# A GpSimd share in the weight split of a mixture-of-experts layer, and an earlier last hidden part

## The chip, the cores and the metric

The kernel runs on one core of one Trainium2 chip. The metric is the device time in microseconds (us) of one execution, the median of several runs. An engine is named here as in the profile: PE is TensorE, DVE is VectorE, ACT is ScalarE, POOL is GpSimd, SP is SyncE (it only issues transfers).

## The reference

Two sub-layers on `x` of 4 x 1024 tokens with 256 numbers each. The first is a cross-attention onto 77 context rows per batch. The second, in which the change lies, is a mixture of nine experts with two picks per token:

```python
x = x + xattn(ctx_1024, layernorm(x), ...)
xf = layernorm(x).reshape(T, H)                          # T = 4096, H = 256
probs = softmax(xf @ Wr)                                 # 9 experts
topk_w, topk_idx = top_k(probs, 2); topk_w /= sum(topk_w)
cw = zeros((T, E)).at[arange(T)[:, None], idxf].add(wf)
gate = silu(einsum('th,ehi->tei', xf, Wg))               # I = 704
hidden = gate * einsum('th,ehi->tei', xf, Wu)
x = x + einsum('tei,eih,te->th', hidden, Wd, cw)
```

## The kernel before

The attention phase (up to about 360 us of the span) sends each token's row to a region of its two experts in device memory. The expert phase then works through 40 tiles of such rows. A **pair** is a tile of 256 rows, a **small tile** one of 128 rows. The small tiles are numbers 6, 11, 16, 20, 25, 30, 34 and 39 of the list `TILES`; 39 is the last of all. So seven small tiles are followed by a pair.

**Number format.** Matmuls run in a rounded float format (`F32R`). To keep precision each operand is split into a rounded part `hi` and a rest `lo = value - hi`, and every product is three matmuls: hi*hi, lo*hi, hi*lo (`product`, lines 341 to 343). ACT makes `hi` (a copy that rounds) and DVE makes `lo` (a subtraction). This holds for the tokens (`tok_t`), for the hidden values (`hid`) and for the weights (`wgt_hi`, `wgt_lo`, made from the loaded `wgt`, or from `spare_wgt` for small tiles).

**Weights of a tile.** They are split in six pieces: `PIECES[0:4]` are gate and up (128 x 704 each), `PIECES[4:6]` are down (128 x 1280, and 128 x 256 of which DVE handles 64 rows). Pieces go two at a time, as parts 0, 1 and 2, through `round_pieces(t, u)` on ACT (line 1113) and `rest_pieces(t, u)` on DVE (line 1961). A tile's pieces are split while the tile ahead of it is computed, into buffer t % 2.

**Order on each engine, written out by hand.**
- PE (`pair_step(t)`): `gate_up(t, 0)`, `gate_up(t, 1)`, `tok_turn(t + 1)` (four transposes, line 1353), `down(t - 1)`, `gate_up(t, 2)`. For a small tile (`single_step(t)`): `single_gate_up(t)`, `tok_turn(t + 1)`, `down(t - 1)`, `hid_turn(t)` (transposes, lines 1471 to 1474).
- ACT and DVE, for each of three inner parts u of a pair: `silu` on ACT, the product `hidden` on DVE (line 1969, for the last part lines 1971 and 1972), weight pieces of tile t + 1, and then the split of the hidden part (`hid_round` on ACT, lines 1148 or 1150 and 1151; `hid_rest` on DVE, lines 1993 or 1996 and 1997). After part 1 the tokens of tile t + 1 are split (`tok_move` line 1098, `tok_rest` line 1945), and ACT writes the result of tile t - 1 (`res_move`, line 1170).
- In a small tile: `single_silu` (line 1142) and `single_hidden` (lines 1981 to 1985), pieces 0, the tokens, pieces 1, `res_move` on ACT, the hidden split (lines 1158 to 1161 on ACT, 2005 to 2008 on DVE), pieces 2.
- POOL, for each tile: `note(t + 2)` (two tiny copies, lines 927 and 928), then `add_results(t)`: wait for the result, one indirect transfer per 128 rows that adds it to the output (line 938), and a wait until these have landed.
- SP: loads of tokens and weights. The down weights of a buffer are loaded anew (`refill_down`) when their split is done.

**What PE waits for.** `gate_up(t, 0)` waits for the first four pieces of tile t (`weights_split`) and for the split tokens (`tok_split`). `down(t)` waits for the last two pieces, for all hidden parts (`hid_ready`) and for a free result bank.

Of the kernel before, what the change touches and what calls it, by code (L numbers as in the profile page):

```python
# [28 lines left out]
P = 128  # L29
# [82 lines left out]
    return 0 if t < EARLY else t % 2  # L112


def pieces_to(t):

    return (t - EARLY) * len(PIECES)

def program(nc, x, ctx_rows, fside, ln1_w, ln1_b, ln2_w, ln2_b, wq, wkv, wout, wr, wg, wu, wd, out):
    valmat_dram = nc.dram_tensor("valmat_dram", (B, H, M, DE), F32).ap()  # L120
# [2 lines left out]
    with ExitStack() as ctx:  # L123
        def sem(name):
            return ctx.enter_context(nc.semaphore(name))
# [321 lines left out]
        tok_split = sem("tok_split")  # L447
        weights_hi = sem("weights_hi")
        weights_split = sem("weights_split")
        hid_made = sem("hid_made")  # L450
        hid_hi = sem("hid_hi")
        pads_zeroed = sem("pads_zeroed")
# [36 lines left out]
            return (early_split, u + 1) if t < EARLY else (weights_split, pieces_to(t) + 2 * KT)  # L489

        def down_split(t):
            return (early_split, UNITS + 2) if t < EARLY else (weights_split, pieces_to(t + 1))

        def tokens_loaded(t):
# [71 lines left out]
        def _(sp):  # L566
# [178 lines left out]
            def refill_down(t):  # L745
                n = TILES[t][1]
                if is_pair(t) and n + WEIGHT_SLOTS < NP:
                    sp.wait_ge(weights_split, pieces_to(t + 1))
                    load_pair_down(n + WEIGHT_SLOTS)
                elif not is_pair(t) and n + 1 < NS:  # L750
                    sp.wait_ge(weights_split, pieces_to(t + 1))
                    load_single_down(n + 1)

            for t in range(EARLY, NT):
# [11 lines left out]
        def _(pool):  # L766
# [163 lines left out]
            for s in range(T + 4):  # L930
                step(s, s)

            def add_results(t):

                i = t % 2
                pool.wait_ge(res_ready, t + 1)
                for a in range(TILES[t][0]):
                    nc.gpsimd.indirect_dma_start(out, bass.IndirectOffsetOnAxis(ap=tok_id[:, t % NOTES, a:a + 1], axis=0),  # L938
                                                 res[i][:, a, :], None, compute_op=ALU.add).then_inc(added, 16)
                pool.wait_ge(added, BLOCKS_TO[t + 1] * 16)  # L940

            pool.wait_ge(tail_row_made, 1)
# [11 lines left out]
        def _(act):  # L954
# [218 lines left out]
            def pair_step(t):  # L1173

                ahead = EARLY - 1 <= t < NT - 1
                src = weights_of(t + 1) if ahead else None
                for u in range(UNITS):
                    silu(t, u)
                    if ahead:
                        round_pieces(t + 1, u, src)  # L1180
                    hid_round(t, u)
                    if u == UNITS - 2 and t:
                        tok_move(t + 1)
                        if t == 2:
                            act.wait_ge(last_stored, 16)
                        res_move(t - 1)

            def single_step(t):

                last = t == NT - 1  # L1190
                src = None if last else weights_of(t + 1)
                single_silu(t)
                if not last:
                    round_pieces(t + 1, 0, src)
                    tok_move(t + 1)
                    round_pieces(t + 1, 1, src)
                res_move(t - 1)
                single_hid_round(t)
                if not last:
                    round_pieces(t + 1, 2, src)  # L1200

            for s in range(T + 4):
                step(s, s)
# [319 lines left out]
        def _(dve):  # L1523
# [487 lines left out]
            def pair_step(t):  # L2011

                src = weights_of(t + 1) if t < NT - 1 else None
                for u in range(UNITS):
                    hidden(t, u)
                    if t < NT - 1:
                        rest_pieces(t + 1, u, src)
                    hid_rest(t, u)
                    if t < NT - 1 and u == UNITS - 2:
                        tok_rest(t + 1)  # L2020

            def single_step(t):
# [6 lines left out]
                    tok_rest(t + 1)  # L2029
                    rest_pieces(t + 1, 1, src)  # L2030
                single_hid_rest(t)
                if not last:
                    rest_pieces(t + 1, 2, src)

            dve.wait_ge(consts_made, 10)
            nc.vector.memset(most[:], 0.0)
# [51 lines left out]
```

## Time and profile before

| | us |
|---|---|
| median of 3 runs (838.15 to 839.69) | 838.44 |
| the profiled execution: its own time | 840.97 |
| the profiled execution: its span, first to last instruction | 839.3 |
| PE busy (95% of the span) | 797.9 |
| DVE busy (80%) | 669.4 |
| ACT busy (74%) | 623.9 |
| POOL busy (45%) | 374.3 |

The span is one execution as the hardware profiler saw it. The execution's own time holds 1.7 us more than the span, around it. Busy shares are averages over phases with different limits; what an engine's idle time costs is seen only where another engine waits for it. In the rows further down, a row without a number in brackets had no idle time worth telling ahead of it. PE's clock was granted in full for nearly all of the span (mean 0.994).

### The profile page before, as it was taken

Reading aid. Unit: us, or ns where it says so; the run is one execution under the profiler, and the core shown is the slowest. Engines: PE = TensorE matmul, PEld = TensorE weight load, DVE = VectorE, ACT = ScalarE, POOL = GpSimd, SP = SyncE. Lnnn points to the kernel's source line nnn. Section 1 sums busy time; section 2 is a strip of 40 time slices with the busy share of each in tenths; the row PEclk is TensorE's granted clock in tenths of the full one; section 3 lists DMA queues with packets and bytes.
Section 4 is the critical chain, followed back from the end, with each engine's and each line's share of the span. In section 5 each row is a group of like instructions: output and inputs, shape, how many; then the busy total and the mean of one; then the engine's idle time right before and its main releaser. Section 6 shows DMA issues by size and latency. Waiting matters only on the chain.

```text
span 839.3 us, 19508 instructions
## 1 busy us (share of the span) xinstructions
PE 797.9 (95%) x6007; PEld 752.6 (90%) x6007; DVE 669.4 (80%) x1624; ACT 623.9 (74%) x1962; POOL 374.3 (45%) x534
## 2 busy tenths in 40 slices
PE   5999999999999999989999999999999999999993
PEld 5846899999999999879999999999999999999993
DVE  6767788888889878888778878788887887888771
ACT  3557889889889888754767777777787777777771
POOL 3020268778777766763324234333333322513232
PEclk9999999999999999999999999999999999999998
DMA  8044731230130121638656283255952654556222
GB/s 288 16 114 134 225 107 39 76 103 27 41 138 30 37 76 39 196 123 203 154 139 161 38 233 77 34 146 149 259 152 46 171 157 113 152 146 158 38 21 25
DMA packets 77675, 96.14 MB, mean 115 GB/s; under 512 B 10311, under 2 KB 64771, under 8 KB 77571
## 3 DMA queue, kind: packets, MB, share of 16 engines
q1 hardware_dynamic: 63811, 75.93, 29.2%
q0 software_dynamic: 13760, 18.96, 12.4%
q8 instruction: 48, 0.79, 0.4%
q14 instruction: 56, 0.46, 0.2%
HBM read 108.14 MB, written 31.29 MB: 166 GB/s over the span
## 4 chain that ended last, share of the span: by engine, by line
PE 83%; DMA 3%; SPq 3%; issue 3%; POOL 2%; DVE 2%; ACT 1%; DVEq 0%; POOLq 0%
PE banks L341 24%; PE banks L342 23%; PE banks L343 23%; PE banks L1339 4%; PE banks L1496 2%; PE banks L1353 2%; PE banks L1295 1%; PE banks L1322 1%; DMA expert_in<-blank 1%; DMA valmat_dram<-val_st 1%; POOL expert_in L875 1%; PE banks L1271 1%; PE banks L1307 1%; SPq L597 1%; DMA wkv_sb<-in_L_xattn_Wkv 0%
## 5 line engine op out<-in xcount | busy, mean ns | idle before, releaser
L341 PE MATMUL banks<-tok_t_hi,wgt_hi 128*128 128x256 f32 x704 | 199.8, 284 | 5.0 <-DVE hid_f L1969 1.9
L343 PE MATMUL banks<-tok_t_hi,wgt_lo 128*128 128x256 f32 x704 | 198.0, 281 | 0.0
L342 PE MATMUL banks<-tok_t_lo,wgt_hi 128*128 128x256 f32 x704 | 197.9, 281 | 0.0
L938 POOL DMA_INDIRECT result<-res,tok_id x72 | 117.7, 1635 | 165.4 <-ACT res L1170 133.8
L1037 ACT ACTIVATE prob<-banks,row_min 128x77 f32<-128x77 f32 x512 | 161.7, 374 | 5.2 <-DVE row_min L1692 5.2
L1961 DVE TENSOR_TENSOR wgt_lo<-wgt,wgt_hi 128x704 fp32r<-128x704 f32 x174 | 150.4, 905 | 14.7 <-ACT wgt_hi L1113 14.7
L341 PEld LDWEIGHTS banks<-tok_t_hi,wgt_hi 128*128 128x128 f32 x704 | 134.3, 191 | 8.1 <-issue 6.0
L343 PEld LDWEIGHTS banks<-tok_t_hi,wgt_lo 128*128 128x128 f32 x704 | 133.6, 190 | 0.0
L342 PEld LDWEIGHTS banks<-tok_t_lo,wgt_hi 128*128 128x128 f32 x704 | 133.4, 190 | 0.0
L1113 ACT ACTIVATE wgt_hi<-wgt 128x704 fp32r (+1 forms) x174 | 130.6, 801 | 0.5
L1037 ACT ACTIVATION_READ_ACCUMULATOR prob<-banks,row_min 128x1 f32 x512 | 130.2, 256 | 0.0
L341 PE MATMUL banks<-wgt_hi,hid_hi 128*128 128x256 f32 x360 | 104.2, 290 | 8.7 <-issue 6.1
L343 PE MATMUL banks<-wgt_hi,hid_lo 128*128 128x256 f32 x360 | 101.3, 281 | 0.0
L342 PE MATMUL banks<-wgt_lo,hid_hi 128*128 128x256 f32 x360 | 101.1, 281 | 0.0
L888 POOL TENSOR_TENSOR prob<-prob,row_inv 128x1232 f32<-128x1232 f32 x32 | 72.1, 2254 | 56.4 <-DVE row_inv L1706 56.3
L341 PE MATMUL banks<-valmat_hi,prob_t_hi 128*128 128x266 f32 x320 | 94.5, 295 | 0.9 <-DVE logits L1714 0.9
L342 PE MATMUL banks<-valmat_lo,prob_t_hi 128*128 128x266 f32 x320 | 91.6, 286 | 0.0
L343 PE MATMUL banks<-valmat_hi,prob_t_lo 128*128 128x266 f32 x320 | 91.5, 286 | 0.0
L875 POOL DMA_INDIRECT expert_in<-xn,top_slot x64 | 67.1, 1048 | 39.0 <-POOL xn L865 25.0
L927 POOL COPY tok_gate<-tok 128x2 f32<-128x2 f32 (+1 forms) x40 | 21.6, 539 | 134.2 <-DMA result<-res,tok_id 130.1
L341 PEld LDWEIGHTS banks<-wgt_hi,hid_hi 128*128 128x128 f32 x360 | 68.2, 190 | 10.9 <-DVE wgt_lo L1961 5.3
L341 PE MATMUL banks<-keymat_hi,zn_t_hi 128*128 128x462 f32 (+1 forms) x192 | 73.4, 382 | 0.0
(272 smaller groups left out, 2105.5 us busy)
## 6 DMA issues: line engine op xcount, KB each, us to landing
wgt<-in_L_ffn_Wg SPq DMA_DIRECT2D x29, 704.0 KB
wgt<-in_L_ffn_Wu SPq DMA_DIRECT2D x29, 640.0 KB
wgt<-in_L_ffn_Wd SPq DMA_DIRECT2D x29, 640.0 KB
tok<-expert_in SPq DMA_DIRECT2D x32, 258.0 KB, 3.9
spare_wgt<-in_L_ffn_Wg SPq DMA_DIRECT2D x9, 704.0 KB, 4.3
spare_wgt<-in_L_ffn_Wu SPq DMA_DIRECT2D x9, 640.0 KB, 5.8
spare_wgt<-in_L_ffn_Wd SPq DMA_DIRECT2D x9, 640.0 KB, 4.3
valmat_f<-valmat_dram SPq DMA_DIRECT2D x4, 1197.0 KB, 6.3
```

Of the source, the lines that this page charges most:

```text
L341: nc.tensor.matmul(to, a[0], b[0], start=first, stop=False)
L342: nc.tensor.matmul(to, a[0], b[1], start=False, stop=False)
L343: return nc.tensor.matmul(to, a[1], b[0], start=False, stop=last)
L875: nc.gpsimd.indirect_dma_start(expert_in, bass.IndirectOffsetOnAxis(ap=top_slot[c % 4][:, k:k + 1], axis=0), xn[c % 4][:, k, :], None).the ...
L888: nc.gpsimd.tensor_tensor(p, p, row_inv[i][:].unsqueeze(2).to_broadcast([P, H, M]), ALU.mult).then_inc(prob_ready, 1)
L927: nc.gpsimd.tensor_copy(tok_gate[:, t % NOTES, 0:blocks], tok[i][:, 0:blocks, GATE])
L938: nc.gpsimd.indirect_dma_start(out, bass.IndirectOffsetOnAxis(ap=tok_id[:, t % NOTES, a:a + 1], axis=0), res[i][:, a, :], None, compute_op ...
L1037: ins = nc.scalar.activation(prob[c % 2][:, h * M:(h + 1) * M], bank[i][:, (h - h0) * M:(h - h0 + 1) * M], ACT.Exp, bias=row_min[c % 2][:, ...
L1113: nc.scalar.activation(wgt_hi[half_of(t)][:, p0:p1], src[:, p0:p1], ACT.Copy).then_inc(weights_hi, 1)
L1339: mm = nc.tensor.transpose(bank[3 + (c * NG + g) % 2][0:n, (m - c0) * P:(m - c0 + 1) * P], prob[c % 2][:, m * P:m * P + n], ident[:])
L1353: mm = nc.tensor.transpose(turned_tokens(t)[:, k, a * P:(a + 1) * P], tok[i][:, a, k * P:(k + 1) * P], ident[:])
L1961: nc.vector.tensor_tensor(wgt_lo[i][0:rows, p0:p1], src[0:rows, p0:p1], wgt_hi[i][0:rows, p0:p1].bitcast(F32), ALU.subtract).then_inc(weig ...
```

## The change

Two things change, both around small tiles.

1. **Down weights of pairs that follow a small tile** (tiles 7, 12, 17, 21, 26, 31, 35; `down_by_pool`). ACT and DVE no longer round and split their two down pieces. POOL does, in `split_down`, which it runs inside `add_results(t - 2)` after issuing the indirect transfers and before waiting for their landing: two copies that round, then two subtractions. PE's `down` and SP's `refill_down` wait for a semaphore of POOL's for these tiles.
2. **The last inner part of a pair in front of a small tile** (`soon`). On ACT `hid_round(t, 2)`, and on DVE `hid_rest(t, 2)`, come ahead of the small tile's weight pieces and no longer behind them.

```diff
+def down_by_pool(t):
+    return EARLY < t < NT and not is_pair(t - 1)
+def pool_downs_to(t):
+    return sum(down_by_pool(i) for i in range(t))
 def pieces_to(t):
-    return (t - EARLY) * len(PIECES)
+    return (t - EARLY) * len(PIECES) - pool_downs_to(t) * len(PIECES[2 * KT:])
...
         def down_split(t):
+            if down_by_pool(t):
+                return pool_down_split, 2 * pool_downs_to(t + 1)
             return (early_split, UNITS + 2) if t < EARLY else (weights_split, pieces_to(t + 1))
...
             def refill_down(t):
                 n = TILES[t][1]
                 if is_pair(t) and n + WEIGHT_SLOTS < NP:
-                    sp.wait_ge(weights_split, pieces_to(t + 1))
+                    sp.wait_ge(*down_split(t))
...
+            def split_down(t):
+                n, i, done = TILES[t][1], half_of(t), 2 * pool_downs_to(t)
+                src = loaded_weights(pool.value_load(tile_table[0:1, 2, n:n + 1], min_val=0, max_val=WEIGHT_SLOTS - 1))
+                pool.wait_ge(*weights_loaded(t, False))
+                for p0, p1 in PIECES[2 * KT:]:
+                    nc.gpsimd.tensor_copy(wgt_hi[i][:, p0:p1], src[:, p0:p1]).then_inc(pool_down_hi, 1)
+                for c, (p0, p1) in enumerate(PIECES[2 * KT:]):
+                    rows = FHALF if c else P
+                    pool.wait_ge(pool_down_hi, done + c + 1)
+                    nc.gpsimd.tensor_tensor(wgt_lo[i][0:rows, p0:p1], src[0:rows, p0:p1],
+                                            wgt_hi[i][0:rows, p0:p1].bitcast(F32), ALU.subtract).then_inc(pool_down_split, 1)
...
             def add_results(t):
...
+                if down_by_pool(t + 2):
+                    split_down(t + 2)
                 pool.wait_ge(added, BLOCKS_TO[t + 1] * 16)
...
             def pair_step(t):          # on ACT; on DVE the same with hid_rest and rest_pieces
...
                 for u in range(UNITS):
                     silu(t, u)
+                    soon = u == UNITS - 1 and not is_pair(t + 1)
+                    if soon:
+                        hid_round(t, u)
                     if ahead:
                         round_pieces(t + 1, u, src)
-                    hid_round(t, u)
+                    if not soon:
+                        hid_round(t, u)
...
             def single_step(t):        # on ACT; on DVE the same with rest_pieces
...
                 single_hid_round(t)
-                if not last:
-                    round_pieces(t + 1, 2, src)
```

**On DVE, from the last part of pair 5 to the hidden split of small tile 6.** In the rows of the order, `spare_wgt` is the small tile's weights and `hid_f` the unsplit hidden part. Line numbers of the changed kernel are some 30 higher. Before:

```order
L1971 TENSOR_TENSOR hid_f<-gate_act,banks 128x256 [waits silu_done]
L1972 TENSOR_TENSOR hid_f<-gate_act,banks 64x256
L1961 TENSOR_TENSOR wgt_lo<-spare_wgt,wgt_hi 128x1280 [waits weights_hi]
L1961 TENSOR_TENSOR wgt_lo<-spare_wgt,wgt_hi 64x256 [waits weights_hi]
L1996 TENSOR_TENSOR hid_lo<-hid_f,hid_hi 128x256 [waits hid_hi]
L1997 TENSOR_TENSOR hid_hi<-hid_f,hid_hi 64x256
```

And in the changed kernel:

```order
L2002 TENSOR_TENSOR hid_f<-gate_act,banks 128x256 [waits silu_done]
L2003 TENSOR_TENSOR hid_f<-gate_act,banks 64x256
L2027 TENSOR_TENSOR hid_lo<-hid_f,hid_hi 128x256 [waits hid_hi]
L2028 TENSOR_TENSOR hid_hi<-hid_f,hid_hi 64x256
L1992 TENSOR_TENSOR wgt_lo<-spare_wgt,wgt_hi 128x1280 [waits weights_hi]
L1992 TENSOR_TENSOR wgt_lo<-spare_wgt,wgt_hi 64x256 [waits weights_hi]
```

The hidden split moved ahead of the two weight pieces; it now stands right behind the product that it splits. Each of the two blocks waits for its rounded part from ACT (`hid_hi`, `weights_hi`).

**On ACT, the same place.** Before:

```order
L1137 ACTIVATE gate_act<-banks 128x256 [waits gu_done]
L1138 ACTIVATE gate_act<-banks 64x256
L1113 ACTIVATE wgt_hi<-spare_wgt 128x1280 [waits down_done,single_d_loaded]
L1113 ACTIVATE wgt_hi<-spare_wgt 128x256
L1150 ACTIVATE hid_hi<-hid_f 128x256 [waits hid_made]
L1151 ACTIVATE hid_hi<-hid_f 64x256
```

And in the changed kernel:

```order
L1166 ACTIVATE gate_act<-banks 128x256 [waits gu_done]
L1167 ACTIVATE gate_act<-banks 64x256
L1179 ACTIVATE hid_hi<-hid_f 128x256 [waits hid_made]
L1180 ACTIVATE hid_hi<-hid_f 64x256
L1142 ACTIVATE wgt_hi<-spare_wgt 128x1280 [waits down_done,single_d_loaded]
L1142 ACTIVATE wgt_hi<-spare_wgt 128x256
```

ACT now waits for DVE's product (`hid_made`) before it rounds the small tile's down pieces.

**On POOL, around the result of pair 5**, in the changed kernel (before it, the rows from `TENSOR_LOAD` to the last subtraction are not there):

```order
L965 DMA result<-res,tok_id 4352x256 [waits res_ready,tok_noted]
L965 DMA result<-res,tok_id 4352x256
L950 TENSOR_LOAD tile_table
L950 ISA x2
L953 ISA [waits wd_loaded0]
L953 COPY wgt_hi<-wgt 128x1280
L953 ISA
L953 COPY wgt_hi<-wgt 128x256
L957 TENSOR_TENSOR wgt_lo<-wgt,wgt_hi 128x1280 [waits pool_down_hi]
L957 TENSOR_TENSOR wgt_lo<-wgt,wgt_hi 64x256 [waits pool_down_hi]
L941 COPY tok_gate<-tok 128x2 [waits tok_loaded0,added]
```

Four data instructions were added between the issue of pair 5's result and the next note; on ACT and DVE the four that did this work for pair 7 are gone.

## Rows read from the trace of the kernel before

**Rows 1.** Page, part 1: busy time, share of the span, number of instructions.
```profile
PE 797.9 (95%) x6007; PEld 752.6 (90%) x6007; DVE 669.4 (80%) x1624; ACT 623.9 (74%) x1962; POOL 374.3 (45%) x534
```

**Rows 2.** Timeline of PE around tile 6: start, duration, engine, instruction, idle before.
```profile
443.15 0.60 PE L1353 MATMUL banks<-ident,tok 128*128 128x128 f32 x4
444.34 0.35 PE L341 MATMUL banks<-wgt_hi,hid_hi 128*128 128x256 f32 x1 [0.59 <-issue]
...
449.14 0.38 PE L341 MATMUL banks<-tok_t_hi,wgt_hi 128*128 128x256 f32 x1
...
454.71 0.60 PE L1353 MATMUL banks<-ident,tok 128*128 128x128 f32 x4
455.07 0.36 PE L341 MATMUL banks<-wgt_hi,hid_hi 128*128 128x256 f32 x1
```

**Rows 3.** Timeline of DVE, pair 5's last part to pair 7's first pieces.
```profile
440.78 0.42 DVE L1972 TENSOR_TENSOR hid_f<-gate_act,banks 64x256 f32<-64x256 f32 x1
441.65 1.82 DVE L1961 TENSOR_TENSOR wgt_lo<-spare_wgt,wgt_hi 128x1280 fp32r<-128x1280 f32 x2 [0.44 <-ACT wgt_hi L1113]
443.39 0.41 DVE L1996 TENSOR_TENSOR hid_lo<-hid_f,hid_hi 128x256 fp32r<-128x256 f32 x1
...
444.27 0.42 DVE L1981 TENSOR_TENSOR single_hid<-single_act,banks 128x256 f32<-128x256 f32 x1
...
447.41 1.68 DVE L1961 TENSOR_TENSOR wgt_lo<-wgt,wgt_hi 128x704 fp32r<-128x704 f32 x2
```

**Rows 4.** Timeline of ACT, the same stretch.
```profile
440.34 1.58 ACT L1113 ACTIVATE wgt_hi<-spare_wgt 128x1280 fp32r<-128x1280 f32 x2
441.82 0.40 ACT L1150 ACTIVATE hid_hi<-hid_f 128x256 fp32r<-128x256 f32 x1
...
442.44 0.74 ACT L1142 ACTIVATE single_act<-banks 128x704 f32<-128x704 f32 x1
```

**Rows 5.** Timeline of DVE while pair 7's gate and up run.
```profile
453.29 0.67 DVE L1969 TENSOR_TENSOR hid_f<-gate_act,banks 128x512 f32<-128x512 f32 x1
453.88 1.68 DVE L1961 TENSOR_TENSOR wgt_lo<-wgt,wgt_hi 128x704 fp32r<-128x704 f32 x2
...
458.89 0.68 DVE L1945 TENSOR_TENSOR tok_t_lo<-banks,tok_t_hi 128x512 fp32r<-128x512 f32 x1
```

**Rows 6.** Timeline of PE where pair 8 begins, and ACT's activation of pair 7.
```profile
459.67 0.36 PE L341 MATMUL banks<-tok_t_hi,wgt_hi 128*128 128x256 f32 x1 [0.21 <-issue]
452.19 0.60 ACT L1135 ACTIVATE gate_act<-banks 128x512 f32<-128x512 f32 x1 [0.48 <-PE banks L343]
```

**Rows 7.** Timeline of ACT and POOL: result of pair 5 and what follows.
```profile
448.60 0.84 ACT L1170 ACTIVATE res<-banks,tok_gate 128x256 f32<-128x256 f32 x2 [2.22 <-PE banks L1496]
450.20 1.57 POOL L938 DMA_INDIRECT result<-res,tok_id  x1 [0.83 <-ACT res L1170]
457.26 1.76 POOL L927 COPY tok_gate<-tok 128x2 f32<-128x2 f32 x1 [2.79 <-DMA result<-res,tok_id]
```

**Rows 8.** By line: duration min/median/max in ns, first and last start, forms.
```profile
L927 POOL COPY tok_gate<-tok x40: 187/362/1978, 366.1 to 807.6; 128x2 f32<-128x2 f32 x32, 128x1 f32<-128x1 f32 x8
L1685 DVE TENSOR_SCALAR xn<-xs,y_mv,y_rstd x32: 402/407/1546, 106.2 to 368.6; 128x256 f32<-128x256 f32 x32
L1727 DVE TENSOR_TENSOR pick<-expert_ids,top_id x32: 177/194/325, 106.6 to 369.1; 128x18 f32<-128x18 f32 x32
```

**Rows 9.** Timeline of POOL and DVE, two places in the attention phase.
```profile
351.88 2.25 POOL L888 TENSOR_TENSOR prob<-prob,row_inv 128x1232 f32<-128x1232 f32 x1 [0.29 <-DVE row_inv L1706]
352.74 1.55 DVE L1685 TENSOR_SCALAR xn<-xs,y_mv,y_rstd 128x256 f32<-128x256 f32 x1
201.25 0.40 POOL L864 COPY xn<-xn 128x256 f32<-128x256 f32 x1
201.35 0.32 DVE L1727 TENSOR_TENSOR pick<-expert_ids,top_id 128x18 f32<-128x18 f32 x1
```

**Rows 10.** Timeline of PE: `down` of pair 38, beside the last small tile.
```profile
819.33 0.36 PE L341 MATMUL banks<-wgt_hi,hid_hi 128*128 128x256 f32 x1 [0.99 <-DVE wgt_lo L1961]
```

More of the change, by code:

```diff
@@ L449, in program @@
         weights_split = sem("weights_split")
+        pool_down_hi = sem("pool_down_hi")
+        pool_down_split = sem("pool_down_split")
         hid_made = sem("hid_made")
@@ L747, in refill_down @@
                 if is_pair(t) and n + WEIGHT_SLOTS < NP:
-                    sp.wait_ge(weights_split, pieces_to(t + 1))
+                    sp.wait_ge(*down_split(t))
                     load_pair_down(n + WEIGHT_SLOTS)
                 elif not is_pair(t) and n + 1 < NS:
-                    sp.wait_ge(weights_split, pieces_to(t + 1))
+                    sp.wait_ge(*down_split(t))
                     load_single_down(n + 1)
@@ L2015, in pair_step @@
                     hidden(t, u)
+                    soon = u == UNITS - 1 and not is_pair(t + 1)
+                    if soon:
+                        hid_rest(t, u)
                     if t < NT - 1:
                         rest_pieces(t + 1, u, src)
-                    hid_rest(t, u)
+                    if not soon:
+                        hid_rest(t, u)
                     if t < NT - 1 and u == UNITS - 2:
@@ L2031, in single_step @@
                 single_hid_rest(t)
-                if not last:
-                    rest_pieces(t + 1, 2, src)
             dve.wait_ge(consts_made, 10)
```

## The prediction

> **What bounds the kernel now.** Read the busy shares first [rows 1]: PE is busy 95% of the span, so only the places where PE stands still can give time back, and any new stand costs time in full. Then the timeline of PE in the expert phase, at the small tiles, and beside each wait the engine that ended it. There are two such places round a small tile, and a third that comes just behind.
>
> First, `down` of the pair ahead. Four transposes begin at 443.15, and `down(5)` begins at 444.34 [rows 2]. The same transposes are followed by `down` after 0.36 us where nothing is waited for (454.71 to 455.07 [rows 2]). So PE stood for 1.19 - 0.36 = 0.83 us. It waited for the hidden split, which DVE ended at about 444.25, just ahead of its next row at 444.27 [rows 3]. This stands ahead of tiles 6, 11, 16, 20, 25, 30 and 34; at tile 39 the stand is 0.99 us [rows 10].
>
> Second, the first matmul of the pair behind the small tile, 449.14 [rows 2]. DVE's last pair of gate and up pieces ends at 447.41 + 1.68 = 449.09 [rows 3], 0.05 us earlier. It is so behind all seven small tiles that have a pair behind them: the distance is 0.05 or 0.06 us each time. PE's wait there is tiny, but it is DVE that sets the start. DVE has no idle time between 441.65 and 449.09.
>
> Third, the first matmul of the pair after that, 459.67 [rows 6], is 0.10 us behind the end of DVE's token split (458.89 + 0.68 = 459.57 [rows 5]), again seven times of seven.
>
> So round each small tile PE and DVE are level, and the bound of these 20 us is the chain on DVE.
>
> **The change, part by part.** All times are those of the trace around tile 6.
>
> *The hidden part first (part 2 of the diff).* DVE's product ends at 440.78 + 0.42 = 441.20 [rows 3]. Before, ACT used this time for the weight pieces, and DVE stood 0.44 us. Now ACT has to wait for the product, rounds the hidden part from 441.23 (0.03 from release to start), and needs 0.31 + 0.40 for its two instructions (two starts take 442.44 - 441.82 = 0.62; the last lasts 0.40 [rows 4]): 441.94. DVE splits it from 441.97, 0.88 us as before (443.39 to 444.27 [rows 3]): 442.85. ACT starts the weight pieces at 441.23 + 0.62 = 441.85. DVE can follow 1.31 us later (440.34 to 441.65 [rows 3, 4]), at 443.16, and is through after 443.39 - 441.65 = 1.74 us, at 444.90.
>
> Two results. `down(5)` finds its hidden part at 442.85 and starts at 443.15 + 0.36 = 443.51: PE's 0.83 us are gone. But DVE reaches the small tile's product at 444.90 and not at 444.27, 0.63 us later, since it now stands 0.77 + 0.31 us where it stood 0.44. All its work up to 449.09 follows without a gap, so this becomes 449.72, and pair 7 starts at 449.77. PE, which would be ready 0.83 us earlier than before, waits 1.4 us there instead. ACT's own work is late by 0.89 us in this stretch, but stays ahead of DVE's. What is late next after the removed wait is thus the second place: **+0.63 us**.
>
> At tile 39 nothing is split for a tile behind, so the gain stays: **-0.99 us**, and the end of the kernel moves with it, as result, transfer and last `down` all follow `down(38)`.
>
> *Down pieces on POOL (part 1).* ACT and DVE lose them. DVE's share, 1.74 us, lay after 449.09, ahead of the product at 453.29; that product waits for PE's matmuls and ACT's activation. ACT had been idle 0.48 us for them [rows 6]. So they bring almost nothing themselves. With pair 7 at +0.63, the activation runs 452.82 to 453.42 and DVE's product starts at 453.45, only 0.16 later than before. From there the same rows take 458.89 - 453.29 = 5.60 us [rows 5], so the token split would run 459.05 to 459.73. PE needs it at about 459.94 (459.67 less its wait of some 0.36, plus 0.63). If POOL disturbed nobody, pair 8 would start 0.27 us late, 0.45 in the three cases where PE ran a little later before.
>
> *Where POOL works.* Pair 5's result on ACT comes 0.83 us earlier than 448.60; POOL's first transfer, 0.76 us behind its end (448.60 + 0.84 to 450.20 [rows 7]), begins at 449.37, two take some 3.4 us, and `split_down(7)` starts at about 453.1 to 453.5. Its work: the subtraction of 128x1280 at the rate of 2.25 us for 1232 [rows 9]: 2.34 us. The copy of 1280: 128x256 takes 0.40 [rows 9], the shortest copy of two elements 0.19 [rows 8]; so 0.19 + 5 x 0.21 = 1.2 us, at most 5 x 0.40 = 2.0. The small two: 0.4 and some 0.6. Together 4.5 us, and they fall on 453 to 459, when DVE is on the path.
>
> *The cost of that.* The trace shows what a long POOL instruction does to DVE. DVE's 128x256 scale takes 0.41 us in the median; the one that began at 352.74 under POOL's multiply (351.88 to 354.13) lasted 1.55 and ended at 354.29, 0.16 behind it [rows 8, 9]. A tiny subtract-like instruction with two inputs in SBUF, 0.18 at best, lasted 0.32 when it met POOL's copy (201.25 to 201.65), and ended 0.02 behind it [rows 9]. The other way round, POOL's copy at 457.26 took 1.76 us in place of 0.19 and ended at 459.02, just as DVE went over to the token split at 458.89, which has only one input in SBUF [rows 5, 7]. DVE's weight pieces and hidden splits all have two inputs in SBUF; the products and the token split read one from PSUM.
>
> So, step by step: the 1.2 us copy begins at 453.1 to 453.5 and holds DVE's pieces, due at 454.05, to 454.3 to 454.7: 0.5 us. DVE then runs pieces (1.6) and hidden split (0.6) without letting POOL in, as at 457.26, until its product at 456.75. There POOL gets its small copy (0.4) and then the subtraction: 457.2 to 459.5. DVE's product ends at 457.35, and the next pieces wait 2.2 us. Then 1.6 + 0.6 + 0.68: the token split ends at 462.4, and pair 8 starts at 462.5, **2.85 us** late, of which 0.63 came with pair 7 (in two cases 0.08 less). PE has full work until the next small tile and gives nothing back; DVE is idle enough later.
>
> The bounds of this: if all four POOL instructions fall on DVE's path (4.5 us), pair 8 is 4.7 us late. If the subtraction gets in only at the token split, it is 0.5 late; undisturbed it is 0.27.
>
> The Trainium skill (page "SBUF — State Buffer", section "Who interferes with whom") has the rule: a VectorE instruction with two SBUF inputs and a GpSimd instruction that reads SBUF exclude each other for a whole instruction, and the first to start wins. The rows above agree (1.55 against 0.41). By it the sum is the one taken here; without it the sum would be the first rival's.
>
> *Others.* `refill_down` of such a pair on SP waits for POOL, some 5 us longer, with a token load behind it; weights are fetched three pairs ahead (23 us or more) and tokens a tile ahead, so this is hidden. POOL's next note comes a few us later, its results are wanted a tile later. Price nothing.
>
> **Sum.** 7 x 2.85 - 0.16 - 0.99 = +18.8 us. The profiled execution took 840.97 (span 839.3 and 1.7 around it), 2.5 more than the median of 838.44. The difference applied to the median gives **857.2 us**.
>
> **Rivals.**
> - *POOL disturbs nobody*, or only where DVE waits anyway. 4 x 0.27 + 3 x 0.45 - 0.99 = +1.4: 839.9 us. For it: the copy may fall wholly into DVE's idle time ahead of 453.45, and small POOL copies passed between two weight pieces without cost. Against: 2.3 us of subtraction do not fit anywhere ahead of the token split. Up to three POOL holds of half size give +8. Chance 0.2 for +0.5 to +8.
> - *Faster.* The second place is not DVE's but PE's own; then 0.83 x 7 come in, 0.36 x 4 and some 0.2 x 3 of the third place, and 0.99: -8.8, 829.6 us. It decides if DVE's 0.63 us delay stays under PE's time. Against: 0.05 us between DVE's end and PE's start, seven times. Chance 0.08.
> - *POOL gets in at every boundary*, and each pair pays the full 4.5 us: 7 x 4.7 - 1 = +32: 870 us. Chance 0.1. POOL lost to DVE at 457.26, which speaks against.
>
> The forecast with its own range (+8 to +27) has 0.62.
>
> **Range.** 840.0 to 868.0 leaves out the faster case, most of the third and a part of the first. A measurement of this kernel tells 0.2% (1.7 us) from no change. Slower by more: 0.82; within: 0.10; faster: 0.08.
>
> **What would show it.** `down` ahead of small tiles follows its transposes after 0.36 us: right for the gain. The first matmul behind a small tile stays 0.05 behind DVE's last piece, and the distance between DVE's product (441.20) and that piece is 0.63 longer. DVE weight pieces at pair 7 last 2 to 4 us in place of 1.68, ending just behind a POOL instruction; the token split of pair 8 is late by 2 to 3 us. POOL's subtraction of 1280 takes 2.3 us. The forecast is wrong if these pieces keep 1.7 us, or if POOL's work starts after the token split.

## The result, and the profile after

The changed kernel takes 880.38 us (median of 4 runs, 880.01 to 882.41); the kernel before took 838.30 in the same comparison (4 runs, 837.34 to 839.69). The ratio is 1.0496, 95% interval [1.0478, 1.0514]: slower by 42.1 us. The forecast was 857.2 with a range up to 868. The direction was right, and so was the place; the loss is 2.2 times the 18.8 us that were forecast.

The page of the kernel after, part 1 and the clock row of part 2 (the granted clock in tenths, 40 slices of the span):

```profile
span 879.1 us, 19508 instructions
PE 808.2 (92%) x6007; PEld 764.7 (87%) x6007; DVE 685.7 (78%) x1610; ACT 611.6 (70%) x1948; POOL 411.3 (47%) x562
PEclk9999999999999999999998999989999999899898
```

Against [rows 1] DVE has 14 instructions less and is busy 16 us longer; PE has the same 6007 instructions and is busy 10 us longer. Neither can be work that was added: DVE's instructions were held, and PE's ran slower in some slices, which the clock row shows as 8.

The waits of PE in the kernel after (sum in us, times, longest) name the two places. A stand is a time in which PE does nothing because it waits:

```profile
PE banks L350 <- DVE tok_t_lo L1976: 26.9, 7, 4.1
PE banks L350 <- DVE wgt_lo L1992: 10.2, 7, 1.5
```

**Around tile 6.** PE first, where the small tile ends and pair 7 begins, and where pair 8 begins. All times of this kernel are in its own span, in which the attention phase ends 1.7 us earlier:

```profile
440.01 0.60 PE L1384 MATMUL banks<-ident,tok 128*128 128x128 f32 x4
440.36 0.36 PE L350 MATMUL banks<-wgt_hi,hid_hi 128*128 128x256 f32 x1
...
444.99 0.27 PE L1505 MATMUL banks<-ident,single_hid 128*64 128x128 f32 x1
446.75 0.38 PE L350 MATMUL banks<-tok_t_hi,wgt_hi 128*128 128x256 f32 x1 [1.48 <-DVE wgt_lo L1992]
...
456.79 0.28 PE L352 MATMUL banks<-tok_t_hi,wgt_lo 128*128 128x256 f32 x1
461.20 0.55 PE L350 MATMUL banks<-tok_t_hi,wgt_hi 128*128 128x256 f32 x1 [4.13 <-DVE tok_t_lo L1976]
461.55 0.41 PE L351 MATMUL banks<-tok_t_lo,wgt_hi 128*128 128x256 f32 x1
```

`down(5)` follows its transposes after 0.35 us where it took 1.19 [rows 2]. Pair 7 starts 0.06 behind DVE's last gate and up piece, as before. Pair 8 starts after a stand of 4.13 us where the stand was 0.21 [rows 6] (over the seven places 3.52 to 4.13), and its first matmuls take 0.55 and 0.41 us where such a one took 0.36 or 0.28.

DVE in the same stretch. The hidden split now stands ahead of the weight pieces:

```profile
438.85 0.43 DVE L2027 TENSOR_TENSOR hid_lo<-hid_f,hid_hi 128x256 fp32r<-128x256 f32 x1 [0.79 <-ACT hid_hi L1180]
439.29 0.42 DVE L2028 TENSOR_TENSOR hid_hi<-hid_f,hid_hi 64x256 fp32r<-64x256 f32 x1
440.02 1.82 DVE L1992 TENSOR_TENSOR wgt_lo<-spare_wgt,wgt_hi 128x1280 fp32r<-128x1280 f32 x2 [0.31 <-ACT wgt_hi L1142]
...
445.01 1.68 DVE L1992 TENSOR_TENSOR wgt_lo<-wgt,wgt_hi 128x704 fp32r<-128x704 f32 x2
...
450.42 0.69 DVE L2000 TENSOR_TENSOR hid_f<-gate_act,banks 128x512 f32<-128x512 f32 x1 [2.63 <-ACT gate_act L1164]
451.21 1.26 DVE L1992 TENSOR_TENSOR wgt_lo<-wgt,wgt_hi 128x704 fp32r<-128x704 f32 x1
452.39 4.70 DVE L1992 TENSOR_TENSOR wgt_lo<-wgt,wgt_hi 128x704 fp32r<-128x704 f32 x1
...
460.42 0.68 DVE L1976 TENSOR_TENSOR tok_t_lo<-banks,tok_t_hi 128x512 fp32r<-128x512 f32 x1
```

The idle times are 0.79 and 0.31, where the prediction had 0.77 and 0.31. The way from DVE's product (its end 438.06) to the end of the last gate and up piece (446.69) takes 8.63 us where it took 7.89: 0.74 more, 0.11 more than forecast. The 0.11 lies in the small tile's pieces, which take 1.85 us to the next instruction (440.02 to 441.87) where they took 1.74 [rows 3]. The reader is to see the pair of pieces at 451.21 and 452.39. Together they last 5.88 us where the same two took 1.68 at 445.01 and in [rows 5]: 4.20 us too long. So it is at all seven pairs (5.42 to 5.88). What POOL does beside them:

```profile
449.87 1.85 POOL L953 CAST wgt_hi<-wgt 128x1280 fp32r x1
451.07 1.64 POOL L953 CAST wgt_hi<-wgt 128x256 fp32r x1
451.80 3.83 POOL L957 TENSOR_TENSOR wgt_lo<-wgt,wgt_hi 128x1280 fp32r<-128x1280 f32 x1
455.24 1.09 POOL L957 TENSOR_TENSOR wgt_lo<-wgt,wgt_hi 64x256 fp32r<-64x256 f32 x1
```

Read the ends. The large copy ends at 451.72 and DVE's first piece 0.75 behind it, at 452.47. POOL's small copy ends 0.24 later (452.71), the large subtraction 2.92 after that (455.63), the small one 0.70 after that (456.33), and DVE's second piece 0.76 behind it (457.09). A piece alone needs some 0.8. So one engine worked while the other was held: DVE ran one piece between POOL's two copies, and then POOL ran three instructions in a row, 3.86 us, while DVE's second piece was held. It is so at five of the seven pairs. At the other two (pieces from 515.37 and from 692.37) POOL began earlier, and what was left of its small copy and both subtractions passed ahead of DVE's first piece, which lasted 4.62 us; the second took 0.88.

**The clock.** Busy time by stretch, kernel after: start and end, length, then busy time and number of instructions of PE, PEld, DVE, ACT and POOL, and last the granted clock, the share of the DMA engines and GB/s:

```profile
440.00:456.00 16.00, 14.52 (x125) 14.24 (x124) 13.20 (x16) 10.20 (x19) 9.69 (x9) 1.00 0.61 146
456.00:461.00 5.00, 1.07 (x10) 0.86 (x8) 5.00 (x7) 2.64 (x6) 2.14 (x4) 0.84 0.00 0
461.00:464.00 3.00, 2.80 (x13) 2.83 (x14) 2.95 (x6) 1.68 (x4) 1.15 (x1) 0.50 0.39 44
464.00:468.00 4.00, 4.00 (x27) 4.00 (x27) 1.16 (x3) 1.42 (x3) 0.31 (x2) 0.72 0.24 66
468.00:480.00 12.00, 12.00 (x104) 12.00 (x104) 8.38 (x13) 8.80 (x17) 3.11 (x2) 1.00 0.21 28
```

While PE stood, its clock fell from 2.4 to 1.2 GHz, and stayed there in the first part of pair 8 (0.50, then 0.72 for a mixture). 13 matmuls ran in the 3 us behind 461, where full speed has some 26. This cost comes on top of the stand itself and was not in the prediction at all. The stand of 1.48 us ahead of pair 7 left the clock at 1.00.

**The sum by places**, in the two profiled spans (879.1 - 839.3 = 39.8). From pair 7's first matmul to pair 8's first: before 10.52 to 10.61, after 14.05 to 14.45, over the seven places +25.8. From pair 8's first matmul to the transposes behind its gate and up: before 5.55 to 5.84, after 6.86 to 8.22, over the seven places +13.2. From the transposes ahead of `down(5)` to pair 7's first matmul: 0.74 more at each place, +5.2 in sum; this is the order of DVE's work. Three things go the other way: the attention phase is 1.7 shorter, PE stood 1.1 us for a token transfer at 420.6 in the profile before and does not in the one after, and the last small tile gains 1.0. Some 0.6 are left.

### The profile page after: what moved, and what is told of

It is laid out like the page before. It is cut to its first block, busy times and chain, and to the rows that moved or that the text cites. A ratio compares the mean times of both kernels' runs of the same rounds, so it can differ in the third digit from the quotient of the medians.

```text
span 879.1 us, 19508 instructions
## 1 busy us (share of the span) xinstructions
PE 808.2 (92%) x6007; PEld 764.7 (87%) x6007; DVE 685.7 (78%) x1610; ACT 611.6 (70%) x1948; POOL 411.3 (47%) x562
## 4 chain that ended last, share of the span: by engine, by line
PE 72%; DVE 13%; issue 4%; ACT 4%; DMA 3%; SPq 1%; DVEq 1%; POOL 1%; ACTq 0%; POOLq 0%
PE banks L350 21%; PE banks L351 21%; PE banks L352 21%; DVE wgt_lo L1992 4%; PE banks L1370 4%; ACT wgt_hi L1142 2%; DMA valmat_dram<-val_st 2%; PE banks L1527 1%; DVE tok_t_lo L1976 1%; DVE hid_lo L2024 1%; PE banks L1384 1%; SPq L611 1%; PE banks L1302 1%; DVEq L1557 1%; PE banks L1338 1%
## 5 line engine op out<-in xcount | busy, mean ns | idle before, releaser
L350 PE MATMUL banks<-tok_t_hi,wgt_hi 128*128 128x256 f32 x704 | 206.9, 294 | 40.0 <-DVE tok_t_lo L1976 26.9
L351 PE MATMUL banks<-tok_t_lo,wgt_hi 128*128 128x256 f32 x704 | 204.4, 290 | 0.0
L352 PE MATMUL banks<-tok_t_hi,wgt_lo 128*128 128x256 f32 x704 | 204.3, 290 | 0.0
L350 PEld LDWEIGHTS banks<-tok_t_hi,wgt_hi 128*128 128x128 f32 x704 | 141.6, 201 | 43.7 <-issue 30.7
L1992 DVE TENSOR_TENSOR wgt_lo<-wgt,wgt_hi 128x704 fp32r<-128x704 f32 (+2 forms) x160 | 165.4, 1074 | 9.9 <-ACT wgt_hi L1142 8.1
L351 PEld LDWEIGHTS banks<-tok_t_lo,wgt_hi 128*128 128x128 f32 x704 | 140.6, 200 | 0.0
L352 PEld LDWEIGHTS banks<-tok_t_hi,wgt_lo 128*128 128x128 f32 x704 | 140.3, 199 | 0.0
L1142 ACT ACTIVATE wgt_hi<-wgt 128x704 fp32r (+3 forms) x160 | 119.6, 797 | 0.5
L1164 ACT ACTIVATE gate_act<-banks 128x512 f32<-128x512 f32 x64 | 37.7, 589 | 55.3 <-PE banks L352 55.3
L1177 ACT ACTIVATE hid_hi<-hid_f 128x512 fp32r<-128x512 f32 x64 | 40.2, 628 | 47.9 <-DVE hid_f L2000 47.8
```

Source lines behind the costliest of these rows:

```text
L350: nc.tensor.matmul(to, a[0], b[0], start=first, stop=False)
L351: nc.tensor.matmul(to, a[0], b[1], start=False, stop=False)
L352: return nc.tensor.matmul(to, a[1], b[0], start=False, stop=last)
L1142: nc.scalar.activation(wgt_hi[half_of(t)][:, p0:p1], src[:, p0:p1], ACT.Copy).then_inc(weights_hi, 1)
L1164: nc.scalar.activation(gate_act[q][:], unit_banks(t, u)[:, :, 0:W], ACT.Silu).then_inc(silu_done, 1)
L1177: nc.scalar.activation(hid[i][0][:, 2 * u:2 * u + 2, :], hid_f[q][:], ACT.Copy).then_inc(hid_hi, 1)
```

## Experiments

The runs of e1 to e4 share one set of runs of the kernel before (838.0 us), e5 to e8 another (838.85), e9 and e10 a third (837.95).

**The order alone.** The second part of the diff on the kernel before; POOL does nothing new:

```diff
+                    soon = u == UNITS - 1 and t < NT - 1 and not is_pair(t + 1)
+                    if soon:
+                        hid_rest(t, u)
                     if t < NT - 1:
                         rest_pieces(t + 1, u, src)
-                    hid_rest(t, u)
+                    if not soon:
+                        hid_rest(t, u)
```

> Part 2 of the change alone: the last hidden part ahead of the small tile's down pieces; ACT and DVE keep all down pieces, POOL has no split. Chain theory: DVE's way from the pair's last product to the last gate and up piece behind the small tile grows by 0.63 us at each of seven small tiles and nothing is given back, because the next start of PE is also DVE's; the last small tile gives 1.0 back: 7 x 0.63 - 1.0 = +3.4, 841.7 us (840 to 843), PE's clock in full. Rival (the order brings the gain and POOL all the loss): 0.83 x 7 and more come in, about 830 us.

Measured: 841.90 us, ratio 1.0047 [1.0033, 1.0062], +3.9. Timeline of PE where pair 7 begins:

```profile
448.12 0.39 PE L341 MATMUL banks<-tok_t_hi,wgt_hi 128*128 128x256 f32 x1 [1.48 <-DVE wgt_lo L1965]
```

The same 1.48 us stand, and pair 8 starts 10.27 or 10.47 later where it was 10.53 or 10.61. So each place costs 0.74 ahead of pair 7 (0.63 forecast) and gives 0.14 to 0.26 back ahead of pair 8 (nothing forecast for this run). The total near the 3.4 expected is in part two deviations that cancel. The order alone is less than a tenth of the 42 us.

**POOL writes but does not read.** The copies and subtractions became memsets of the same places (ahead of the subtraction's a second one):

```diff
-                    nc.gpsimd.tensor_copy(wgt_hi[i][:, p0:p1], src[:, p0:p1]).then_inc(pool_down_hi, 1)
+                    nc.gpsimd.memset(wgt_hi[i][:, p0:p1].bitcast(F32), 0.0).then_inc(pool_down_hi, 1)
```

> The changed kernel, but POOL fills the down regions with zeros (five memsets, about the same number of instructions, some 4.5 us) in place of copying and subtracting: it leaves out the values of these down weights. POOL instructions that only write SBUF. Port theory: nothing holds DVE any more, its pair of pieces at pair 7 lasts 1.7 and not 5.9 us, PE does not stand 4 us, its clock stays in full: +1.4 to +3 over the kernel before, 840 to 842 us. Rival (POOL's time in itself, its place in its queue or the late semaphore costs): above 860 us.

Measured: 840.54 us, ratio 1.0030 [1.0019, 1.0042]. POOL, and below it DVE:

```profile
451.68 2.01 POOL L954 MEMSET wgt_hi<- 128x1280 f32 x2
453.50 1.29 POOL L959 MEMSET wgt_lo<- 128x1280 f32 x1
454.85 1.42 POOL L961 MEMSET wgt_lo<- 128x1280 f32 x2
...
452.32 0.69 DVE L2003 TENSOR_TENSOR hid_f<-gate_act,banks 128x512 f32<-128x512 f32 x1 [2.72 <-ACT gate_act L1167]
453.11 1.69 DVE L1995 TENSOR_TENSOR wgt_lo<-wgt,wgt_hi 128x704 fp32r<-128x704 f32 x2
```

DVE's pieces keep 1.69 us right beside 4.5 us of POOL's work. The kernel leaves out the values of these weights, but it has the same order, and about the same time on POOL. So it is not that POOL is late, nor that DVE and ACT lost instructions, nor POOL's writes: its reads hold DVE. This is the Trainium skill's rule too ("SBUF — State Buffer", section "Who interferes with whom": two inputs in SBUF collide with a GpSimd instruction that reads it, not with one that only writes it), and the trace agrees.

**Keep PE at work in the stand.** 34 matmuls with an overwritten result, ahead of pair 8's wait for DVE's token split:

```diff
+            def keep_busy(t):
+                pe.wait_ge(res_ready, t - 2)
+                hi = gate_up_of(wgt_hi[(t - 1) % 2])
+                for _ in range(FILLERS):
+                    nc.tensor.matmul(bank[6 + (t - 1) % 2][:, 0:W], hi[:, 0, 0:P], tok_t[(t - 1) % 2][0][:, 0, :], start=True, stop=True)
...
+                if down_by_pool(t - 1):
+                    keep_busy(t)
```

> The changed kernel with 34 matmuls that nobody reads (256 columns, about 4 us) on PE in the seven places where it stands 4 us, ahead of the wait. Clock theory: the stand by itself lowers PE's clock to 1.2 GHz for 3.4 or 6.8 us behind it, which costs 1.3 to 2.4 us each, 13 us in sum; with PE kept busy the clock stays and the time is 867 us (865 to 870). Rival (the slow stretch behind the stand comes from elsewhere, the weights or PE's queue): 880 us or a little more.

Measured: 869.03 us, ratio 1.0372 [1.0357, 1.0387]. The stretches that answer to those above:

```profile
457.00:461.50 4.50, 4.50 (x41) 4.50 (x39) 4.50 (x8) 2.68 (x6) 1.64 (x3) 1.00 0.00 0
461.50:465.00 3.50, 3.50 (x30) 3.39 (x30) 3.39 (x7) 1.84 (x5) 1.28 (x3) 1.00 0.32 37
```

The same POOL work, the same hold on DVE, 238 matmuls more, and 11.4 us less than the change (880.38): that is the clock's part.

**Down pieces later, on DVE and ACT.** On the kernel before, without POOL's part. The down pieces of the pair behind a small tile go behind the token split in that pair's second part, those of the small tile behind its own hidden split, so the last hidden split of the pair ahead follows its product at once, as in e1. The down pieces have semaphores of their own:

```diff
-                    if t < NT - 1:
+                    if t < NT - 1 and (u < UNITS - 1 or is_pair(t + 1)):
                         rest_pieces(t + 1, u, src)
...
                         tok_rest(t + 1)
+                        if after_small(t):
+                            rest_pieces(t, UNITS - 1, weights_of(t))
...
                 single_hid_rest(t)
                 if not last:
-                    rest_pieces(t + 1, 2, src)
+                    rest_pieces(t, 2, weights_of(t))
```

> The kernel before without POOL's split: the small tile's down pieces go behind its hidden split (where those of the pair behind stood), and the pair's own down pieces behind the token split in its second part, both on ACT and DVE; down pieces have semaphores of their own. Chain theory: 1.74 us leave DVE's chain between the pair's last product and the last gate and up piece, PE's 0.83 us at seven places go, the start behind the small tile follows PE, and the third place keeps its distance; the last small tile gains less: 829.5 us (828 to 833). Rival (DVE's order is not what PE is level with): 838 us.

Measured: 835.07 us (12 runs, 832.62 to 838.31), ratio 0.9962 [0.9947, 0.9976]: a gain, but 5.6 us less than expected, and outside the expected range. Waits of PE:

```profile
PE banks L1367 <- DMA tok<-expert_in: 2.8, 2, 1.7
```

Before it was 1.1 us, once. The small tile's weights are split later, so SP's refill is issued later, and the token load stands behind it in SP's queue: behind tile 16 it is issued 11.5 us after the pair's first matmul (570.07 and 558.61), where it was 5.0 (568.25 and 563.28). These 2.8 us are at most half of what was missed; the rest stays open. "Price nothing" for what SP's queue carries holds for the change, where PE waits for no token load, but not for any later release.

**The POOL part alone**, in the old order:

```diff
-                    soon = u == UNITS - 1 and not is_pair(t + 1)
+                    soon = False
```

> Part 1 of the change alone: POOL splits the down pieces as in the changed kernel, the last hidden part stays behind the small tile's pieces. Theory (port hold with all four POOL instructions in a row, and the clock behind the stand): the hold and the slow clock stay at all seven places, only the order's part goes, which was worth about +3.4: 876 us (872 to 880). Rival (hold and order need each other, as POOL starts earlier in relation to DVE with the new order): 860 us or less.

Measured: 888.38 us, ratio 1.0592 [1.0573, 1.0610]: more than the whole change, and outside both what was expected and the rival. DVE and POOL:

```profile
451.24 0.69 DVE L2000 TENSOR_TENSOR hid_f<-gate_act,banks 128x512 f32<-128x512 f32 x1 [1.75 <-ACT gate_act L1164]
452.03 6.58 DVE L1992 TENSOR_TENSOR wgt_lo<-wgt,wgt_hi 128x704 fp32r<-128x704 f32 x2
...
451.40 2.84 POOL L953 CAST wgt_hi<-wgt 128x1280 fp32r x2
453.32 4.53 POOL L957 TENSOR_TENSOR wgt_lo<-wgt,wgt_hi 128x1280 fp32r<-128x1280 f32 x2
```

The pieces last 6.58 us in place of 5.88. POOL's first copy starts 0.16 behind DVE's product; in the full change it started 0.55 ahead of it. Its 1.85 us thus lie 0.7 more beside DVE's pieces. So the new order, which costs 0.74 by itself ahead of pair 7, brings the result and with it POOL's work forward and makes the hold smaller: the two parts help each other, where I had added them. PE stands 4.7 to 5.5 us there.

**POOL's two copies without the subtractions** (two columns of memset in their place):

```diff
-                    nc.gpsimd.tensor_tensor(wgt_lo[i][0:rows, p0:p1], src[0:rows, p0:p1],
-                                            wgt_hi[i][0:rows, p0:p1].bitcast(F32), ALU.subtract).then_inc(pool_down_split, 1)
+                    nc.gpsimd.memset(wgt_lo[i][0:rows, p0:p0 + 2].bitcast(F32), 0.0).then_inc(pool_down_split, 1)
```

> The changed kernel with POOL's two rounding copies, but its two subtractions replaced by writing two columns: it leaves out the rest part of these down weights. Theory: the port is held only for the copies, DVE's pair of pieces at pair 7 lasts about 2.5 to 3.3 us in place of 5.9, PE stands some 0.8 to 1.3 us, too short to lower its clock: 846 us (843 to 851). So most of the loss is the 3.8 us subtraction. Rival (any long POOL instruction with reads costs the full stand): above 865 us.

Measured: 842.43 us, ratio 1.0044 [1.0027, 1.0061], no more than the order alone, and below the expected range. DVE and POOL:

```profile
450.45 2.86 POOL L953 CAST wgt_hi<-wgt 128x1280 fp32r x2
...
451.92 2.14 DVE L1991 TENSOR_TENSOR wgt_lo<-wgt,wgt_hi 128x704 fp32r<-128x704 f32 x2
```

The copies hold DVE 0.46 us here (2.14 - 1.68), 0.14 to 0.57 over the seven places. That is the 0.5 of the prediction, and less than the 0.8 to 1.6 that this run was expected to show. Pair 8 is 0.05 to 0.55 later than in e1, and PE stands 0.50 us at most ahead of it.

**The subtractions on POOL without the copies**, which ScalarE makes:

```diff
-                for p0, p1 in PIECES[2 * KT:]:
-                    nc.gpsimd.tensor_copy(wgt_hi[i][:, p0:p1], src[:, p0:p1]).then_inc(pool_down_hi, 1)
...
+                    for p0, p1 in PIECES[2 * KT:]:
+                        nc.scalar.activation(wgt_hi[half_of(t + 1)][:, p0:p1], src[:, p0:p1], ACT.Copy).then_inc(pool_down_hi, 1)
```

> As the change, but ScalarE makes the two copies of the down weights that follow a small tile (behind its hidden rounding, as before the change), and GpSimd only the two subtractions. Theory (a subtraction of GpSimd with two inputs in SBUF keeps VectorE's weight pieces out as long as it and the instruction behind it last): the subtractions begin about when VectorE's gate and up pieces are due and hold them some 2 to 3 us; pair t+2 is 2 to 3 us late in place of 3.7, with or without the clock's fall behind it: 855 to 872 us, likeliest 862. Rival (it is the unbroken run of four instructions that gets GpSimd in, and two alone fall into VectorE's idle time): 842 to 847 us.

Measured: 863.52 us, ratio 1.0299 [1.0276, 1.0322]. POOL and DVE, each instruction by itself:

```profile
451.04 3.57 POOL L955 TENSOR_TENSOR wgt_lo<-wgt,wgt_hi 128x1280 fp32r<-128x1280 f32 x1
453.97 2.05 POOL L955 TENSOR_TENSOR wgt_lo<-wgt,wgt_hi 64x256 fp32r<-64x256 f32 x1
...
452.38 3.06 DVE L1994 TENSOR_TENSOR wgt_lo<-wgt,wgt_hi 128x704 fp32r<-128x704 f32 x1
455.37 1.41 DVE L1994 TENSOR_TENSOR wgt_lo<-wgt,wgt_hi 128x704 fp32r<-128x704 f32 x1
```

The turns, by ends: large subtraction 454.61, DVE's first piece 455.44, small subtraction 456.02, DVE's second piece 456.78. Here DVE did get in between the two subtractions. It is so at five of the seven places; at the other two (513 and 683) both subtractions passed ahead of DVE's first piece. The pieces are held 2.7 us here, 2.2 to 2.7 in all. Apart, copies and subtractions hold these pieces 0.46 and 2.7 us; together it was 4.2, so the parts do not add up. PE then stands 2.0 to 2.65 us, and pair 8 starts 12.5 to 13.0 behind pair 7. In five of the seven places pair 8's first part then took 7.1 to 7.3 us, and in two 5.8: there the clock stayed.

**The split one result later:**

```diff
-                if down_by_pool(t + 2):
-                    split_down(t + 2)
+                if down_by_pool(t + 1):
+                    split_down(t + 1)
```

> The changed kernel with POOL's split one result later: behind the transfer of the small tile's own result, about 12 us behind the pair's start and not 3. Same instructions. Port theory: no hold in front of the token split, so no stand of PE there; the same 4 us now fall on DVE's last product, pieces and hidden split of the pair, which PE's down wants at 16.7 us; DVE has some 1 us of slack there, so PE stands 2 to 3 us at down in seven places, again with the slow clock behind it in most: 860 to 875 us. Rival (the loss belonged to the place in front of the token split alone): 841 us.

Measured: 865.36 us, ratio 1.0318 [1.0301, 1.0335]. Pair 8 is on time (10.27 or 10.47), but `down(7)` now waits:

```profile
466.06 0.36 PE L350 MATMUL banks<-wgt_hi,hid_hi 128*128 128x256 f32 x1 [2.37 <-issue]
```

The row says that the profile shows no releaser. DVE's last work for pair 7 in that stretch:

```profile
459.59 5.61 DVE L1992 TENSOR_TENSOR wgt_lo<-wgt,wgt_hi 128x1280 fp32r<-128x1280 f32 x2 [0.55 <-ACT wgt_hi L1142]
465.54 0.42 DVE L2028 TENSOR_TENSOR hid_hi<-hid_f,hid_hi 64x256 fp32r<-64x256 f32 x1
```

The stretches around it:

```profile
463.40:466.00 2.60, 0.29 (x3) 0.05 (x1) 2.56 (x4) 0.00 (x0) 2.16 (x4) 1.00 0.00 0
466.00:468.00 2.00, 1.94 (x10) 1.97 (x11) 2.00 (x3) 1.29 (x3) 0.00 (x0) 0.60 0.00 0
```

DVE's two pieces last 5.61 us where such a pair took 1.82 [rows 3], and its hidden split ends at 465.96, 0.10 ahead of `down(7)`; POOL's own split of the down weights had ended at 464.90. So moving POOL's work away from the token split moves the hold to DVE's last hidden split, for which `down` waits. PE stands 2.35 to 2.50 us, and the clock falls behind it in six of the seven places. Neither of the two places tried has room for the work on POOL.

**The POOL part alone, with PE kept at work** (e5 and 42 of the filling matmuls of e3):

```diff
+FILLERS = 42
```

> GpSimd's part of the change alone, in the old order (888.4 us), with 42 extra matmuls on PE, of 128 columns by 256, ahead of the wait in front of the gate and up of the pair behind the pair that follows a small tile; their result is overwritten. Theory (of the 49 us, 7 x 4.7 = 33 are VectorE held by GpSimd, the rest is the clock at half speed behind PE's stand): the clock stays, 872 us (868 to 876). Rival (the extra over the full change is more holding of VectorE, not clock): above 880 us.

Measured: 872.09 us, ratio 1.0402 [1.0379, 1.0424]. Of the 49.5 us of e5, some 16 are the clock (888.38 - 872.09), and the other 33 are DVE held, 4.7 for each of seven. The same division of the change, with e3, is 11.4 and 31. So of the 8 us by which e5 was above the whole change, some 5 are the clock and 3 the hold.

**Down pieces between.** As e4, but the small tile's own down pieces stand between the last gate and up piece and the small tile's hidden split:

```diff
                     rest_pieces(t + 1, 1, src)
+                    rest_pieces(t, 2, weights_of(t))
                 single_hid_rest(t)
-                if not last:
-                    rest_pieces(t, 2, weights_of(t))
```

(and the same on ScalarE)

> As e4, but the small tile's down pieces go between the last gate and up piece and the small tile's hidden split, where DVE stood 1.25 us in e4 and ACT 2 us. Theory: DVE is no longer level with PE at the token split (0.3 us at seven places), and the small tile's down weights are loaded anew some 2 us earlier, so the token loads that PE waited for in three places (1.1, 1.7 us) come in time: 2 to 5 us less than e4, 830 to 833 us. Rival: no change from e4.

Measured: 829.72 us, ratio 0.9897 [0.9880, 0.9913]: 9.1 us faster than before, the fastest of all, and just below the expected 830 to 833. PE and DVE:

```profile
440.44 0.60 PE L1366 MATMUL banks<-ident,tok 128*128 128x128 f32 x4
440.80 0.36 PE L349 MATMUL banks<-wgt_hi,hid_hi 128*128 128x256 f32 x1
...
445.43 0.27 PE L1487 MATMUL banks<-ident,single_hid 128*64 128x128 f32 x1
445.46 0.39 PE L349 MATMUL banks<-tok_t_hi,wgt_hi 128*128 128x256 f32 x1
...
443.73 1.68 DVE L1974 TENSOR_TENSOR wgt_lo<-wgt,wgt_hi 128x704 fp32r<-128x704 f32 x2
445.33 1.81 DVE L1974 TENSOR_TENSOR wgt_lo<-spare_wgt,wgt_hi 128x1280 fp32r<-128x1280 f32 x2
```

DVE ends the last gate and up piece at 445.41, and PE starts pair 7 at 445.46 straight behind its transposes. The same two parts of work, moved past the two places where PE waits for DVE but kept on DVE, remove both stands.

## Why the prediction was wrong

**What held.** PE's 0.83 us ahead of `down(5)` went, PE stood 1.48 us ahead of pair 7 (1.4 in the prediction), and the 0.99 us at the last small tile went (`down(38)` follows its last matmul after 0.17 us). "If POOL disturbed nobody" had +1.4; e2 measured +2.5. The place (DVE's weight pieces of pair 7) and the mechanism (POOL's reads) were right. The row with 1.55 us against 0.41 [rows 9] is a scale of one tensor, so it showed that POOL holds DVE, but nothing of two inputs. The trace after shows these: DVE's product at 450.42, with one input in SBUF, keeps 0.69 us beside POOL's copy, while the pieces with two are held.

**The step that failed first** is in "the cost of that": "DVE then runs pieces (1.6) and hidden split (0.6) without letting POOL in, as at 457.26, until its product". It rests on one row, a POOL copy of two elements held for 1.76 us [rows 7]. In the trace DVE ran one piece and then had to let three POOL instructions pass, 3.86 us (at two of seven pairs they passed ahead of its first piece). The rule that the prediction cites from the Trainium skill ("SBUF — State Buffer", section "Who interferes with whom"), that the first to start wins for a whole instruction, does not say who is next when both have work waiting; I filled that from the row that suited. The third rival, in which each pair pays for all of POOL's work (7 x 4.7 - 1 = +32), is what happened but for the clock: e3 is +31. I gave it 0.1.

**Mis-sized terms.** The large subtraction was 2.34 us; by the ends of the trace it is 2.92, and in e9, where it comes first and DVE's piece finds it at work, the next instruction starts 2.93 behind it and its record lasts 3.57. The row that I scaled [rows 9] is a multiply whose second operand is one column. The Trainium skill ("GPSIMD Engine Reference", section "3.1 Elementwise — side-by-side cycle accounting") has 2.6 cycles of 1.2 GHz per element for two inputs; an estimate from it for 1280 elements is 2.8 us, nearer than mine. The large copy was 1.2: the next one does start 1.20 behind it (449.87 to 451.07), but its record, and with it the hold, lasts 1.85. The hold of a pair of pieces was 3.74 to 4.20 in place of 0.5 + 2.2. PE lost 3.5 to 3.9 us for each pair behind pair 7's start, where the prediction had 2.85 - 0.63 = 2.2: over seven, 25.8 in place of 15.5. And DVE's chain ahead of pair 7 became 0.74 us longer, not 0.63.

**The term that was missing** is the clock. The prediction had "PE has full work until the next small tile and gives nothing back", at full speed. PE stood 4 us, and ran at 1.2 GHz behind it: +13.2 by the intervals, 11.4 by e3. Without the clock the result would have been 869, just outside the range of 840 to 868. With the hold as forecast the clock would have cost too: in e9, where PE stood 2.0 to 2.65 us, pair 8's first parts took 7.7 us more in sum, which by an estimate gives 865, still inside. The two errors together miss the range by 12.

**What stays open.** Why POOL's small subtraction passed DVE's waiting piece in the full change, though its record starts 2.85 us after the piece's (452.39 and 455.24), and did not at five of seven places in e9, where it starts 1.59 after it, but did at the other two, at some 1.0: no run tells these apart. And 1.3 us of e1: by places its trace shows 5.2 - 1.6 - 1.0 = +2.6, its runs +3.9; the profiled execution of the kernel before was itself 2.5 over its median.

## What to carry to other kernels

When work goes to GpSimd that reads SBUF, add all of its instructions to VectorE's chain as the upper bound if VectorE's own instructions there have two inputs in SBUF; one row in which VectorE won says nothing on who wins next. Where an edit makes PE stand for some us (2.0 to 4.1 here), price PE's clock behind the stand too, here 12 us beside 26. Look first for a place a few us later on the same engines: that gave 1% here, without a new engine.

## What the runs showed of the hardware

- The clock fell to 1.2 GHz at PE stands of 3.52 to 4.13 us in the full change (7 of 7), of 4.7 to 5.5 in e5 (7 of 7), of 2.35 to 2.50 in e7 (6 of 7) and of 2.00 to 2.65 in e9 (5 of 7), and not at those of 1.4 to 1.5 us ahead of pair 7 (0 of 7). Pair 8's first part then took up to 2.4 us longer in the full change, and up to 2.7 in e5.
- Instructions of POOL and DVE that both read SBUF, DVE's with two inputs there, run one after the other, whole: a piece of DVE that needs some 0.8 us ends 0.75, 0.76, 0.83 and 0.76 behind the end of POOL's that it waited for.
- The record of such an instruction includes what it waited: 3.83 us for the large subtraction where DVE's piece had held the small copy ahead of it, 3.15 where none had (515.38), and 4.70 for a piece that needs 0.8. So busy time, DVE's 16 us more above all, is no measure of work here.
